# Turning the first ten token tiles on TensorE, and M = Wq Wkᵀ built as its weights land

## The reference, cut to what matters

```python
x = x + attn(layernorm(x), W, b)          # x: 2 x 8192 x 1024, causal, one head of 1024
x = x + moe(layernorm(x), ...)            # 8 experts, top 2, and a shared gated MLP

def attn(x, W, b):
    q, k, v = split(einsum('btc,cd->btd', x, W) + b, 3)
    weights = einsum('btc,bTc->btT', q, k) / sqrt(1024)
    weights = where(lower triangle, weights, -9e15)
    return einsum('btT,bTc->btc', softmax(weights), v)
```

## Time and profile before

| | us |
|---|---|
| median of 3 runs | 1337.18 (1337.04 to 1341.15) |
| the profiled execution, device time | 1337.72 |
| its span on the slowest core (core 7) | 1336.2 |
| spans of the other cores | 1319.4 to 1332.3 |
| PE busy | 1145.8 (86% of the span) |
| DVE, ACT, POOL busy | 574.1, 466.1, 265.2 |

### The profile page before, as it was taken

The page is one execution under the profiler, slowest core; times in us unless marked ns, Lnnn a source line. Parts: engine busy times, 40 slices in busy tenths (PEclk is TensorE's granted clock), DMA queues, the critical chain, the costliest instruction groups (busy, mean ns, idle before and its releaser), DMA issues.

```text
span 1336.2 us, 18688 instructions; the slowest of 8 cores (1319.4 to 1336.2 us)
## 1 busy us (share of the span) xinstructions
PE 1145.8 (86%) x6280; PEld 580.3 (43%) x6280; DVE 574.1 (43%) x1273; ACT 466.1 (35%) x900; POOL 265.2 (20%) x435
## 2 busy tenths in 40 slices
PE   4678879778989898996978578699996999999887
PEld 1355445323434343442433233244563666666433
DVE  2354335335656665665674754312111111111466
ACT  2244233324543543644545443421321332222200
POOL 4101102111021112023121031360021222121431
PEclk9889889888989999998989879899998999999988
DMA  9936434997666766778959577599199999999977
GB/s 166 227 74 129 118 64 72 248 243 168 123 161 141 166 144 149 152 160 198 196 118 187 91 129 111 96 170 165 44 211 215 206 213 220 221 207 207 313 262 264
DMA packets 258828, 225.43 MB, mean 169 GB/s; under 512 B 197156, under 2 KB 203428, under 8 KB 258728
## 3 DMA queue, kind: packets, MB, share of 16 engines
q0 software_dynamic: 52848, 129.02, 45.4%
q1 hardware_dynamic: 205880, 95.14, 33.4%
HBM read 172.22 MB, written 51.38 MB: 167 GB/s over the span
## 4 chain that ended last, share of the span: by engine, by line
PE 53%; DMA 17%; DVE 12%; ACT 8%; issue 6%; SPq 3%; POOL 1%; DVEq 0%; ACTq 0%; POOLq 0%
PE po L605 11%; PE po L1114 8%; PE sp L1089 8%; PE sp L790 7%; PE sp L542 7%; DMA PT<-P 5%; PE po L1174 4%; PE po L484 4%; DVE per_unit L560 3%; DMA XT<-XN 3%; PE po L666 2%; DMA O<-xkv 2%; ACT P L572 2%; DMA Y<-ys 2%; DMA gb<-Y,lohi 2%
## 5 line engine op out<-in xcount | busy, mean ns | idle before, releaser
L605 PE MATMUL po<-XN,PT 128*128 128x512 bf16 x1088 | 259.3, 393 | 50.6 <-DMA PT<-P 40.8
L542 PE MATMUL sp<-XT,QT 128*128 128x512 bf16 x1088 | 255.0, 387 | 25.6 <-DMA XT<-XN 24.6
L605 PEld LDWEIGHTS po<-XN,PT 128*128 128x128 bf16 x1088 | 107.7, 101 | 193.3 <-issue 79.8
L542 PEld LDWEIGHTS sp<-XT,QT 128*128 128x128 bf16 x1088 | 106.2, 99 | 155.6 <-issue 38.2
L1127 DVE COPY ys<-po 128x1024 f32<-128x1024 f32 x35 | 42.9, 1224 | 229.8 <-PE po L1114 207.0
L790 PE MATMUL sp<-QT,WGU 128*128 128x512 bf16 x512 | 117.2, 390 | 5.9 <-DVE HB L805 5.5
L570 ACT ACTIVATE per_unit<-nm,s_q 128x1 f32<-128x1 f32 x72 | 21.2, 295 | 256.9 <-DVE nm L567 105.4
L618 DVE SCALAR_TENSOR_TENSOR O<-O,per_unit,po 128x512 f32<-128x512 f32 x112 | 80.5, 742 | 55.5 <-PE po L605 54.1
L484 PE MATMUL po<-XT,M 128*128 128x256 bf16 x512 | 65.3, 291 | 28.8 <-DMA XT<-XN 15.7
L1096 ACT ACTIVATE hT<-sp 128x640 bf16<-128x640 f32 x64 | 45.1, 704 | 113.4 <-PE sp L1089 113.4
L560 DVE TENSOR_REDUCE per_unit<-sp 128x1 f32<-128x1024 f32 (+1 forms) x72 | 83.4, 1158 | 1.6
(11 more groups left out here) (147 smaller groups left out, 1321.3 us busy)
## 6 DMA issues: line engine op xcount, KB each, us to landing
Y<-ys SPq DMA_DIRECT2D x40, 512.0 KB, 8.9
O<-xkv POOLq DMA_DIRECT2D x64, 256.0 KB, 5.7
xs<-xkv POOLq DMA_DIRECT2D x60, 256.0 KB, 3.9
G<-zero POOLq DMA_DIRECT2D x8, 1280.0 KB, 7.7
xn<-G SPq DMA_DIRECT2D x8, 1280.0 KB, 20.7
xr<-xkv POOLq DMA_DIRECT2D x16, 512.0 KB, 4.9
W<-w1p POOLq DMA_DIRECT2D x32, 256.0 KB, 16.4
W<-w2p POOLq DMA_DIRECT2D x32, 256.0 KB, 21.1
```

Source lines behind the costliest of these rows:

```text
L542: fn = lambda e, d=d, h=h: e.matmul(sp[j][:, h * 512:h * 512 + 512], QT[:, d * 2048 + t * 128:d * 2048 + t * 128 + 128], XT[kb % 2][:, h * ...
L605: fn = lambda e, c=c, h=h, i=i: e.matmul(ring[i], PT[p][:, c * 128:c * 128 + 128], XN[kb % 2][:, c * 1024 + h * 512:c * 1024 + h * 512 + 5 ...
```

## The change

**Loads.** `kv[0, 4]` is loaded with the first four tiles, second in order. A table of 128 x 128 ones on the diagonal (`ident0`, 32 KB) is loaded next on SP's queue, and the mask, `iota8` and `tri` behind it. SP then waits for `d_wk[1]` before it issues the loads of `kv[0, 5..7]`, and `own[2]`, `own[3]`.

**Turning.** The ten tiles `kv[0, 0..7]`, `own[2]`, `own[3]` are normalised on DVE (`ln_norm(jb, True)`, L274, one operation), turned by eight PE transposes into a PSUM bank, and taken from there to `XT` by one ACT operation (`pe_turn`). Their DMA transposes are gone. The first five (`lead`) are turned in bank 7 while M's left half is built: tile 0 behind part `c` = 3, the next behind 5, 6 and 7, the last behind the evictions of the left half. The other five (`second`) are turned in the ring banks 4 to 6: three behind `project(0)`, two behind `qk(1)`.

**M.** The left half is built in banks 0 to 6 as parts land, its eighth row block afterwards in bank 7. The right half is also built part by part, in banks 0 to 6, then come the bias products in bank 7, and the eighth row block of the right half in bank 0. All evictions stand together behind their matmuls.

**Statistics.** Those of tiles 5, 6 and 7 are handed out inside `project(0)`, between its DVE evictions; those of `own[2]` and `own[3]` follow it.

```diff
-    for j in range(4):
+    for j in (0, 4, 1, 2, 3):
         ln_load(kv[0, j], SP)
...
-    first = ln_steps([kv[0, j] for j in range(4)])
-    for s in first:
-        s()
-    for j in range(4, 8):
+    k_id0 = SP.dma(lambda e: e.dma_start(out=ident0[:], in_=idenh), d_const[8])
+    k_mask = SP.dma(lambda e: e.dma_start(out=mask[:], in_=maskh), d_const[1])
...
+    SP.wait((d_wk[1].sem, 16))
+    for j in (5, 6, 7):
         ln_load(kv[0, j], SP)
     ln_load(own[2], SP)
     ln_load(own[3], SP)
...
+    def pe_turn(jb, b, free):
+        PE.wait(jb["normed"], k_id0, free)
+        for d in range(8):
+            fn = lambda e, d=d: e.transpose(bank_bf[b][:, d * 128:d * 128 + 128],
+                                            jb["xn"][:, d * 128:d * 128 + 128], ident0[:])
+            if d < 7:
+                PE.quiet(fn)
+        k = PE.do(fn)
+        jb["turned"] = ACT.do(lambda e: e.activation(
+            out=jb["xt"], in_=bank_bf[b].rearrange("p (d n) -> p d n", d=8), func=AF.Identity), k)
+        return jb["turned"]
...
+    lead = [kv[0, j] for j in (0, 4, 1, 2, 3)]
+    free7 = None
+    for i in range(len(lead) + 1):
+        if i < len(lead):
+            ln_stats(lead[i])
+        if i > 0:
+            ln_norm(lead[i - 1], True)
+    turn_at = {3: [0], 5: [1], 6: [2], 7: [3]}
     for c in range(8):
         PE.wait((d_wq[c].sem, 32))
...
+        for r in range(7):
+            mm_m(0, r, r, c)
+        for i in turn_at.get(c, []):
+            free7 = pe_turn(lead[i], 7, free7)
+    m_free = [evict_m(0, r, r, r % 2) for r in range(7)]
+    free7 = pe_turn(lead[4], 7, free7)
+    PE.wait(free7)
+    for c in range(8):
+        mm_m(0, 7, 7, c)
+    free7 = evict_m(0, 7, 7, True)
+    for c in range(8):
+        PE.wait((d_wk[c].sem, 16))
+        for r in range(7):
+            if c == 0:
+                PE.wait(m_free[r])
+            mm_m(1, r, r, c)
+    m_free = [evict_m(1, r, r, r % 2) for r in range(7)]
...
-    project(0)
+    second = [kv[0, 5], kv[0, 6], kv[0, 7], own[2], own[3]]
+    project(0, [lambda: ln_stats(second[0]), lambda: None, lambda: ln_stats(second[1]), lambda: ln_norm(second[0], True),
+                lambda: ln_stats(second[2]), lambda: ln_norm(second[1], True)])
+    ln_norm(second[2], True)
+    for jb in second[:3]:
+        i = ring_n[0] % 3
+        ring_n[0] += 1
+        ring_free[i] = pe_turn(jb, 4 + i, ring_free[i])
...
+    for jb in second[3:]:
+        ln_stats(jb)
+        ln_norm(jb, True)
...
             qk(x)
+            if x == 1:
+                for jb in second[3:]:
+                    i = ring_n[0] % 3
+                    ring_n[0] += 1
+                    ring_free[i] = pe_turn(jb, 4 + i, ring_free[i])
```

More of the change, by code:

```diff
@@ L147, in build_program @@
     bvs = at("bvs", 512, F32, 196608)
+    ident0 = at("ident0", 128, BF16, 190464)
     singles = small("singles", 8)
@@ L396, in mm_m @@
[L396 to L400, removed]
+    bank_bf = [v.bitcast(BF16) for v in bank]
+    def pe_turn(jb, b, free):
[9 more added lines that the diff above has]
+        return jb["turned"]
@@ new lines, in build_program, with mm_m, evict_m @@
+    m_tok = {}
+    def mm_m(h, r, b, c):
+        fn = lambda e: e.matmul(bank[b], WQT[:, c * 1024 + r * 128:c * 1024 + r * 128 + 128],
+                                WKT[:, c * 1024 + h * 512:c * 1024 + h * 512 + 512], start=(c == 0), stop=(c == 7))
+        if c == 7:
+            m_tok[h, r] = PE.do(fn)
+        else:
+            PE.quiet(fn)
+    def evict_m(h, r, b, on_act):
+        dst = M[:, r * 1024 + h * 512:r * 1024 + h * 512 + 512]
+        if on_act:
+            return ACT.do(lambda e: e.activation(out=dst, in_=bank[b], func=AF.Identity, scale=1.0 / 32.0), m_tok[h, r])
+        return DVE.do(lambda e: e.tensor_scalar(out=dst, in0=bank[b], scalar1=1.0 / 32.0, scalar2=None,
+                                                op0=ALU.mult), m_tok[h, r])
@@ L433, in build_program @@
+    PE.wait(free7, k_bb, k_ones)
     for o, W_, s0 in ((0, WKT, 0), (1, WQT, 8)):
@@ L436, in build_program @@
                 fn = lambda e, d=d, c=c, o=o, W_=W_, s0=s0: e.matmul(
-                    bank[o][:, d:d + 1], W_[:, c * 1024 + d * 128:c * 1024 + d * 128 + 128],
+                    bank[7][:, 8 * o + d:8 * o + d + 1], W_[:, c * 1024 + d * 128:c * 1024 + d * 128 + 128],
                     bqk_bf[:, s0 + c:s0 + c + 1], start=(c == 0), stop=(c == 7))
[L439 to L442, removed]
+                PE.quiet(fn)
     for c in range(8):
-        fn = lambda e, c=c: e.matmul(bank[2][:, 0:1], ones[:], bb_bf[:, c:c + 1], start=(c == 0), stop=(c == 7))
+        fn = lambda e, c=c: e.matmul(bank[7][:, 16:17], ones[:], bb_bf[:, c:c + 1], start=(c == 0), stop=(c == 7))
         if c == 7:
@@ L448, in build_program, with project @@
             PE.quiet(fn)
-    k_u = DVE.do(lambda e: e.tensor_scalar(out=u_sb[:], in0=bank[0][:, 0:8], scalar1=1.0 / 32.0, scalar2=None,
-                                           op0=ALU.mult), k_uw)
-    k_w = DVE.do(lambda e: e.tensor_scalar(out=w_bf[:], in0=bank[1][:, 0:8], scalar1=1.0 / 32.0, scalar2=None,
-                                           op0=ALU.mult))
[L453 to L457, removed]
+    PE.wait(m_free[0])
+    for c in range(8):
+        mm_m(1, 7, 0, c)
+    k_start = m_tok[1, 7]
+    k_u = DVE.do(lambda e: e.tensor_scalar(out=u_sb[:], in0=bank[7][:, 0:8], scalar1=1.0 / 32.0, scalar2=None,
+                                           op0=ALU.mult), k_b0)
+    k_w = DVE.do(lambda e: e.tensor_scalar(out=w_bf[:], in0=bank[7][:, 8:16], scalar1=1.0 / 32.0, scalar2=None,
+                                           op0=ALU.mult))
+    k_b0 = DVE.do(lambda e: e.tensor_scalar(out=b0, in0=bank[7][:, 16:17], scalar1=1.0 / 32.0, scalar2=None,
+                                            op0=ALU.mult))
+    k_M7 = evict_m(1, 7, 0, True)
+    k_Mv, k_Ma = m_free[6], k_M7
+    m_free[0], free7 = k_M7, k_b0
+    sp_free = [m_free[0], m_free[3]]
+    sp_wait0 = [m_free[1], m_free[2]]
     ring_free = [m_free[4], m_free[5], m_free[6]]
     ring_n = [0]
-    misc_free = [m_free[7]]
+    misc_free = [free7]
     qt_ready = {}
     sq_ready = {}
-    def project(p):
+    def project(p, between=()):
         if p == 0:
@@ L498, in project @@
             toks.append(ring_free[i])
+            for s in between[d2:d2 + 1]:
+                s()
         qt_ready[2 * p] = qt_ready[2 * p + 1] = toks
@@ L536, in qk @@
         j = x % 2
-        PE.wait(sp_free[j], sp_wait0[0] if x == 0 else None)
+        PE.wait(sp_free[j], *(sp_wait0 if x < 2 else []))
         PE.wait(*qt_ready[t])
@@ L824, in build_program @@
     fillers = {72: [(0, 0)], 73: [(0, 1)], 74: [(0, 2), (1, 0)], 75: [(1, 1)], 76: [(1, 2)], 77: [(2, 0), (2, 1)], 78: [(2, 2)]}
-    project(0)
+    second = [kv[0, 5], kv[0, 6], kv[0, 7], own[2], own[3]]
[6 more added lines that the diff above has]
+        ring_free[i] = pe_turn(jb, 4 + i, ring_free[i])
+    k_bvr0 = DVE.do(lambda e: e.tensor_copy(bvr[:], bvs[:]), *[(d_const[4 + i].sem, 16) for i in range(4)])
+    k_bvr = DVE.do(lambda e: e.tensor_tensor(out=bvr[64:128, :], in0=bvs[64:128, :], in1=bvr[64:128, :],
+                                             op=ALU.subtract), k_bvr0)
+    p_free[2] = k_bvr
+    k_e640 = DVE.do(lambda e: e.tensor_scalar(out=e640[:], in0=iota8[:], scalar1=float(CAP), scalar2=None,
+                                              op0=ALU.mult), k_iota)
+    k_taken = [DVE.do(lambda e: e.tensor_copy(taken[:], e640[:]), k_e640)]
+    for jb in second[3:]:
+        ln_stats(jb)
+        ln_norm(jb, True)
     x = 0
@@ L846, in build_program @@
             xr_free[0] = k_zero
+            POOL.wait(own[3]["turned"])
             load_xr(0)
@@ L910, in build_program @@
     d_xn, d_ident = slots("xn", 2)
-    bank_bf = [b[:].bitcast(BF16) for b in bank]
     def load_rows(queue, ex, *after):
```

18 lines of the change are left out of this document (3 added, 15 removed).

## The result

The changed kernel is slower: its time is 1.0069 of the kernel before on the same chip (interval 1.0039 to 1.0098), and 1.0090 (1.0055 to 1.0126) when both were timed again later. Of the 1337.18 us of before, that is +9.2 and +12 us. The forecast was +6.6. The medians themselves were 1349.62 against 1341.1 and 1362.18 against 1347.11; the ratios leave out disturbed executions, most of them with the cores of a die at a visibly lower clock, and the medians do not. The profiled execution of the changed kernel took only 1338.69, against 1337.72 for the one before, so I read the ratios and, inside the trace, the times of single steps. Rows of after are of core 7 where nothing else is said, as those of before.

The account below looks back on a forecast made before the run. The bound was the chain through M's last ACT eviction, `project(0)`, unit 0's mask and `project(1)`, whose end shifts the whole span. Terms -5.2 + 5.4 + 6.4 = +6.6 gave 1344.3 us, range 1336 to 1350.

Parts of the forecast that it names:

- E1: End of `project(1)`, 97.38 us before; its shift was taken to be the shift of the whole span.
- Steps 1 and 2: Up to `project(0)`: PE waits for late `ident0`, then builds M; start at 68.0 instead of 73.20, -5.2 us.
- Step 3: From `project(0)` to unit 0's mask: added statistics and normalising on DVE make it 17.1 us instead of 11.65, +5.4.
- Step 4: From unit 0's mask to E1: `project(1)` waits for two ACT copies and loses its overlap, +6.4 us.
- rival (b): Normalising at 1.28 us instead of 0.69, eighth row block at half clock: +4.4, 1348.7 us; chance 0.13.
- (a): Front of M: `ident0` overtakes the tiles and is there in time, 5 us shorter, 1339.3 us; chance 0.20.
- (c): Front's gain kept, own tiles 4 and 5 normalised in DVE's and ACT's gaps: 1332.5 us; chance 0.10.

Follow-up runs that it names:

- bias products early: Changed kernel with its 136 one-column bias matmuls moved into the right half of M, behind its second part; project(2) at 106.7 us, no ratio given.
- the table alone: Changed kernel with only `ident0` issued ahead of the tiles; project(0) at 66.7 us, project(2) at 118.9 us, no ratio given.

## Why the prediction was right or wrong

**Direction and mechanism held.** M is used sooner, its work comes back on DVE, `project(1)` loses its overlap, and E1's shift reaches the end. The size was too small: +6.6 by the sum, +10.0 at `project(2)` on core 7 and on the mean of the cores. Term by term on core 7, E1 moved by -5.5 + 8.1 + 7.5, where the sum had -5.2 + 5.4 + 6.4. The terms that failed are those of steps 3 and 4, 2.7 and 1.1 us too small, and half clock is 2.25 and 1.1 of that.

**Steps 1 and 2 were right to 0.3 us.** First turn 32.96 (33.2 forecast), eighth row block 47.18 (47.2), right half 48.90 to 60.99 (49.0 to 61.4), `project(0)` 67.71 (68.0): -5.5 instead of -5.2. Some of this is luck. The right half and the bias products took 0.7 us less than forecast (12.09 and 3.40 against 12.4 and 3.8), the last row block 0.7 more (2.48 against 1.8, the clock falling), and the second execution of the same kernel has `project(0)` at 68.8 on the mean.

**Step 3 failed in one sentence**, "PE no longer starts cold". The mask came 19.8 us after `project(0)`, +8.1 instead of +5.4. Core 5 of the same execution, whose clock did not fall, has it at 85.33 - 67.79 = 17.54. So have the two other such cores, within 0.01, and all eight cores of the kernel with the bias products early; the five whose clock fell have 19.5 to 19.9. The forecast was 17.1. So 2.25 of the 2.7 us too little are the clock. DVE's timeline, core 7, shows it in the evictions of `project(0)`:

```profile
69.75 0.48 DVE L519 TENSOR_SCALAR QT<-po,u_sb 128x256 bf16<-128x256 f32 x1 [4.80 <-PE po L507]
...
72.86 0.48 DVE L519 TENSOR_SCALAR QT<-po,u_sb 128x256 bf16<-128x256 f32 x1 [1.12 <-PE po L507]
...
83.67 0.81 DVE L274 TENSOR_SCALAR XN<-xs,mvr 128x1024 bf16<-128x1024 f32 x1 [0.79 <-ACT mvr L263]
```

The first eviction comes 2.04 us after `project(0)`'s start, not 1.1, and DVE waits for PE before the second. The normalising was 0.79 to 0.81, nearer to my 0.69 than to rival (b)'s 1.28; that the Trainium skill (VectorE: DVE Perf Modes, section The perf-mode tier table) gives it a higher rate than an operation with two tensors agrees with 0.80 against 1.279 for as many elements in the earlier trace rows, though not by the full factor of two; the operation of that row (SCALAR_TENSOR_TENSOR) is not itself in the table. The two waits of 0.79 for ACT's roots I had counted in the 3.0 us of an own tile.

**Step 4**: from the mask to `project(1)`'s start 10.34 us, as forecast (8.3 + 2.04). The matmuls then took 9.70, not the 8.57 I had taken from `project(0)` before: the granted clock was still 0.50 at 101 to 102, while before it was full 3.0 us after the start. +7.5 instead of +6.4, a term mis-sized. (The sum in the prediction has 10.65 for 2.04 + 8.57, which is 10.61; the +6.4 stays.) E1 to `project(2)`: 13.05, as forecast (13.2), but that is no constant: on the three cores whose clock did not fall in `project(0)` it is 14.0 to 14.5. From `project(0)` to `project(2)` these take 51.4 to 51.9 us and the other five 52.7 to 53.2, so of the 2.25 us only some 1.3 are left at `project(2)`. Why is not shown.

**The rivals.** (a) is refuted in its premise by 22.7 us, and in its price: with the table in time, the table alone was worth 1 to 2 us, not 5, because I had not read ACT's list for what stands ahead of the first copy. (b) was right that half clock would add, but in the profiled execution not where: the eighth row block took 1.89 us, at the full clock. In the second execution it took 2.9 to 3.6 us on four of eight cores, as (b) had it. (c) needed ACT at its two copies within 20 us of `project(0)`; it came there after 28.1 (95.78).

## What to carry to other kernels

When work that stood in front of a wait is moved behind it, price it where it lands: what matters is whether the next bound step waits for the same engine's list, not whether that engine is idle on average. Before pricing the removal of a wait, write down what stands second in each list that the waiting step needs; here three such waits (table, roots, weights) lay behind one another, and the 9 us of the first were worth 1 to 2. Judge the parts of a front by marks on all cores, since 0.5% is hard to tell from one time.

## What the runs showed of the hardware

One-column matmuls, back to back, kept PE busy for 3.40 of 3.40 us at the full granted clock, and within 1.5 us of their end the clock fell to 0.50 on five of eight cores in both executions of the changed kernel, and on seven of eight in both kernels that place them inside the right half. There it was full again well before `project(0)` (by 61.50 on the core shown). In the seven other executions that have them in front of the last row block and `project(0)` it fell on two to six of eight cores, and in the two of the changed kernel not on the same five, so the program alone does not settle which cores lose it. That PE shows no gap is no proof that it keeps its clock.
